# Two blocks of a two-layer network on one core: the scatter-adds of the second stretch read their row numbers from the loaded rows, loads run six blocks ahead instead of eight, and the last sum goes in two transfers instead of four

## The reference, cut to what matters

```
t = xf * rsqrt(mean(xf * xf) + EPS) * norm_w
vals, idx = top_k(t @ gate_w.T + gate_b, 4);  gates_k = softmax(vals)
h = einsum('mh,eoh->emo', t, w1) + b1          # 16 experts, 256 -> 512
a = minimum(h[..., ::2], 7);  b = clip(h[..., 1::2], -7, 7)
act = a * sigmoid(1.702 * a) * (b + 1)
y = einsum('emi,edi->emd', act, w2) + b2       # 256 -> 256
out = x + sum over the 4 experts of a token of gate * y
```

## Time and profile before

| | |
|---|---|
| time, median of 3 runs | 1045.91 us (1045.18 to 1046.28) |
| the profiled execution | 1043.59 us, of which its instructions span 1041.7 us |
| PE busy over the span | 970.5 us (93%) |
| POOL busy over the span | 427.1 us (41%) |
| second stretch on PE, first to last h_mm | 844.7 to 1010 us |

### The profile page before, as it was taken

One profiled execution on the slowest core, in us unless ns is written; L12 is line 12 of the kernel. 1 busy time (PEld: TensorE's weight loads), 2 busy tenths in 40 slices (PEclk: granted clock), 3 DMA queues, 4 the chain that ended last, 5 costly groups with the idle time before them and its releaser, 6 DMA issues.

```text
span 1041.7 us, 20507 instructions
## 1 busy us (share of the span) xinstructions
PE 970.5 (93%) x6020; PEld 820.9 (79%) x6020; DVE 722.6 (69%) x2545; ACT 671.3 (64%) x1944; POOL 427.1 (41%) x450
## 2 busy tenths in 40 slices
PE   6999999999999999999999999996888799999990
PEld 4669888887988888888888888884677689999980
DVE  3564775777677678677867867776867668888870
ACT  2657786687677767757866776782735456676650
POOL 3322431342362353154236225224064555665673
PEclk9999999999999999999999999998999899999995
DMA  9928993994789210020012004057177699998954
GB/s 307 307 80 301 376 371 113 375 377 164 278 293 376 96 62 1 18 88 31 1 62 73 2 1 165 3 183 264 52 188 169 188 247 217 225 226 215 225 133 81
DMA packets 93725, 180.53 MB, mean 173 GB/s; under 512 B 9949, under 2 KB 29085, under 8 KB 92717
## 3 DMA queue, kind: packets, MB, share of 16 engines
q1 hardware_dynamic: 73467, 148.55, 43.1%
q0 software_dynamic: 18800, 30.30, 12.9%
q10 hardware_dynamic: 1346, 0.36, 0.2%
HBM read 77.71 MB, written 107.99 MB: 178 GB/s over the span
## 4 chain that ended last, share of the span: by engine, by line
PE 86%; DVE 4%; issue 3%; ACT 2%; DMA 2%; POOL 1%; SPq 0%; ACTq 0%; DVEq 0%; POOLq 0%; another core or an unknown queue 0%
PE bank L1076 12%; PE bank L1040 11%; PE bank L1012 10%; PE bank L1085 6%; PE bank L1030 5%; PE bank L1002 5%; PE bank L991 4%; PE bank L962 3%; PE bank L868 3%; PE bank L1031 3%; PE bank L1001 3%; PE bank L1021 3%; PE bank L877 3%; PE bank L946 2%; PE bank L984 2%
## 5 line engine op out<-in xcount | busy, mean ns | idle before, releaser
L1076 PE MATMUL bank<-RB 128*128 128x128 f32 x1264 | 157.8, 279 | 6.1 <-issue 3.8
L1076 PEld LDWEIGHTS bank<-RB 128*128 128x128 f32 x1264 | 150.6, 195 | 9.6 <-issue 4.6
L1871 POOL TENSOR_TENSOR RB<-RB 128x512 f32<-128x512 f32 x64 | 67.6, 1056 | 203.1 <-DVE RB L1650 203.1
L1040 PE MATMUL bank<-RA,RB 128*128 128x256 f32 x512 | 133.7, 383 | 1.1 <-DVE X L1690 0.8
L1341 ACT ACTIVATE RB<-RA,nw 128x512 f32 x158 | 105.5, 715 | 37.2 <-issue 16.5
L1012 PE MATMUL bank<-RA 128*128 128x256 f32 x512 | 121.2, 380 | 0.0
L1012 PEld LDWEIGHTS bank<-RA 128*128 128x128 f32 x512 | 95.2, 190 | 15.0 <-issue 2.9
L1040 PEld LDWEIGHTS bank<-RA,RB 128*128 128x128 f32 x512 | 91.0, 190 | 15.5 <-issue 4.7
L1847 POOL TENSOR_TENSOR qs<-qs,half 128x4 f32<-128x4 f32 x64 | 64.9, 1014 | 93.1 <-DVE qs L1659 79.6
L1085 PE MATMUL bank<-RB,BC 128*128 128x256 f32 x316 | 83.2, 387 | 3.3 <-DVE BC L1777 2.3
L1242 ACT ACTIVATE RB<-bank 128x256 f32<-128x256 f32 x128 | 48.7, 381 | 57.9 <-PE bank L1031 52.8
(11 more groups left out here) (251 smaller groups left out, 2387.3 us busy)
## 6 DMA issues: line engine op xcount, KB each, us to landing
xsD<-BC SPq DMA_DIRECT2D x17, 4232.0 KB, 33.0
RB<-in_w2b SPq DMA_DIRECT2D x79, 256.0 KB
RB<-xsD SPq DMA_DIRECT2D x62, 264.5 KB
BC<-modD SPq DMA_DIRECT2D x16, 512.0 KB, 4.2
X<-xsD SPq DMA_DIRECT2D x17, 264.5 KB, 3.4
RA<-in_w SPq DMA_DIRECT2D x2, 2048.0 KB, 8.0
RA<-in_w SPq DMA_DIRECT2D x6, 512.0 KB, 11.5
RA<-in_L_attn_Wq SPq DMA_DIRECT2D x1, 2048.0 KB, 13.8
```

Source lines behind the costliest of these rows:

```text
L1040: m = pe.matmul(bank[5][:, t * 256:t * 256 + 256], OT[:, u % 2, t * 128:t * 128 + 128], Wo[:, h, :], start=(h == 0 and t == 0), stop=(h == ...
L1076: m = pe.matmul(ps[:, 128 * j:128 * j + 128], WS[:, n % 2, c, 128 * j:128 * j + 128], XT[:, n % 2, c * 128:c * 128 + 128], start=(c == 0), ...
L1871: pool.tensor_tensor(sq, qrow, qrow, ALU.mult).then_inc(mine("q_sq", p), 1)
```

## The change

In the second stretch `tok` is gone. `y_add` takes the token numbers straight from column 256 of the loaded rows. The rows' slot must then stay untouched until the add has read it and landed, so `xb(n)` now waits for `y_add(n - 11)` in place of `y_out(n - 11)` and `tok(n - 11)`, and the loads are listed six blocks ahead instead of eight. The first stretch keeps its copies. `merge` covers the same bytes in two transfers of 1 MB.

```diff
-    lo, hi, ahead = FIRST, NBLK, 8
+    lo, hi, ahead = FIRST, NBLK, 6
...
-        if lo <= n - 1 < hi:
-            p.add("tok", n - 1)
...
-    p.add("merge", by=16 * 4)
+    p.add("merge", by=16 * 2)
...
                     if n >= FIRST + RINGS[1]:
-                        on.wait_ge(*done("y_out", n - RINGS[1]))
-                        on.wait_ge(*done("tok", n - RINGS[1]))
+                        on.wait_ge(*done("y_add", n - RINGS[1]))
...
             def y_add(n):
                 on.wait_ge(*done("y_out", n))
-                on.wait_ge(*done("tok", n))
+                if n < FIRST:
+                    on.wait_ge(*done("tok", n))
+                else:
+                    on.wait_ge(*done("xb", n))
...
-                pool.indirect_dma_start((out_r, accD)[n % 2], bass.IndirectOffsetOnAxis(to[:, n % 6:n % 6 + 1], 0), YB[n % 5], None,
+                places = to[:, n % 6:n % 6 + 1] if n < FIRST else rows(n)[:, 256:257].bitcast(U32)
+                pool.indirect_dma_start((out_r, accD)[n % 2], bass.IndirectOffsetOnAxis(places, 0), YB[n % 5], None,
...
-                for i in range(4):
-                    pool.dma_start(out_r[512 * i:512 * i + 512, :].rearrange("(a c) n -> a (c n)", c=8), accD[512 * i:512 * i + 512, :].rearrange("(a c) n -> a (c n)", c=8),
+                for i in range(2):
+                    pool.dma_start(out_r[1024 * i:1024 * i + 1024, :].rearrange("(a c) n -> a (c n)", c=8), accD[1024 * i:1024 * i + 1024, :].rearrange("(a c) n -> a (c n)", c=8),
```

## The result

The changed kernel takes **1048.61 us** (median of 12 runs, 1046.62 to 1054.21), the kernel before 1045.07 (12 runs beside them, 1044.02 to 1047.83). The ratio is 1.0039, with a 95% interval of 1.0027 to 1.0050: about 4 us slower. (A ratio is taken over the timed runs as a whole. It is not the quotient of the two medians, and differs from it by up to 0.07%.) The profiled execution took 1048.47 us with a span of 1046.7. That of the kernel before took 1043.59, which is 1.5 us under the median of 1045.07, so the two profiles stand 4.9 us apart where the medians stand 3.5.

A forecast was written before the change was run, and what follows sets the result against it. It took the adds' chain of landings, then POOL's pace and the DMA-bound merge, as the bound. Terms -0.4 - 0.3 + 0.5 + 0.3 = +0.1, less half the even adds' small gains, gave 1045.7 us; range 1042.6 to 1049.4.

The forecast's parts named there:

- rival A: Second stretch: landings get slower as loads start together with adds; 0.2 us a step, 4.6 us, 1050.3 us; chance 0.23.
- The step by which A was to be told: Odd adds from block 27 to 71: 6.0 us a step and up would show rival A, 5.9 no change.
- What bounds the kernel: Blocks 27 to 73: add, landing, add, landing, twice side by side; then POOL's pace for five adds, then the merge.
- The six microseconds by which the last add stood behind the last y_out: Kernel's end: last y_out written 1014.66, last add starts 1020.68; taken as the adds' backlog, so the end hangs on them.
- The 2.73 us that an add takes "with the engines idle": Last add's landing time with idle engines, set against some 5 us in the loaded stretch.
- The new wait of SP: SP's row loads wait for an add's landing, some 3 us later each round; cost nothing, bounds 0 to 0.5 us.
- Where the loads' traffic goes: Last row loads run later, beside the last odd adds; 0.5 us lost, between 0 and 1.5.
- The tail: Adds 73 to 78 without copies, at 1.88 us start to start; together 0.4 us saved.
- The merge: Final sum in two transfers, first one slower to start; 0.3 us later, between -0.4 and +1.5.
- The first weights: Start of second stretch: asked for 2.2 to 2.4 us sooner, y_mm(21) loses its 0.28 us wait; 0.3 us saved.
- 6.0 and up is A: Sign in the profile: an odd adds' step of 6.0 us or more, block 27 to 71, means rival A.
- from 0.09 us a step on: Added time per odd adds' step, over 23 steps, from which rival A would decide the result.

The follow-up runs named there:

- e4_merge2: The kernel before with only the merge changed, to two transfers of 1 MB instead of four of 512 KB; 1044.17 us, ratio 0.9993.
- e7_three_targets: The changed kernel with second-stretch adds going in turn to three arrays, the third never summed; 1040.26 us against 1044.41, ratio 0.9967.
- e13: The changed kernel with thirteen row slots and the transposes of x in blocks 60 to 69 done three times over; 1045.23 us, ratio 1.0027.
- e15: The changed kernel with thirteen row slots and the transposes of x in blocks 50 to 69 done three times over; 1046.22 us, ratio 1.0047.
- e2_wait_add: The kernel before with row loads six ahead and waiting for y_add(n - 11) to land, copies and four merge transfers kept; 1050.16 us, ratio 1.0046.
- e1_ahead6: The kernel before with row loads six blocks ahead instead of eight, nothing else; 1046.37 us against 1044.81, ratio 1.0019.
- e3_slots13: The changed kernel with 13 row slots instead of 11, so loads wait for the add of block n - 7; 1045.04 us, ratio 1.0006.
- e12: The changed kernel with twelve row slots, rows seven ahead, five weight slots and w2x three ahead; 1044.29 us against 1042.04, ratio 1.0019.

## Why the prediction was wrong

It said 1045.7 us and no change that can be told; the kernel is 0.39% slower, in the manner of rival A, and near the size given there (4.6 us; some 4 measured). The step by which A was to be told has 6.11 - 5.89 = 0.22 in the two profiles, but 5.89 was a quick execution, and against the 6.00 of `e4_merge2` it is 0.11.

**What bounds the kernel** was read rightly: the adds' chain of landings, with PE near beside it. Loosening the chain gave 0.33 to 0.4% against before. But it was put too absolutely, and a view spoke against that: I read the end of the chain that ended last, and its stretch from 870 to 1005 us, which I did not weigh, is PE's. The six microseconds by which the last add stood behind the last y_out were read as backlog. 3.7 of them are there even where PE is the bound (1012.84 to 1016.56 in `e7_three_targets`), since the last five adds leave POOL 1.85 us apart; the backlog left at the end of the profile before was 2.3. And a backlog covers PE only until it is used up (e13, e15).

One reading of a row was wrong beside that. The 2.73 us that an add takes "with the engines idle" is the time of an add that moves nothing. In the kernel before, while adds 74 to 77 run:

```profile
1012.00:1020.00 8.00, 1.13 (x4) 0.68 (x4) 2.08 (x6) 0.00 (x0) 7.36 (x9) 0.69 0.04 1
```

1 GB/s is 8 KB in 8 us, where 128 rows of 1 KB would be 128 KB an add: these adds move no rows. So 2.73 against 5 compares idle with busy engines and no rows with 128, both at once.

**"The new wait of SP ... nothing, with 0 to 0.5 as bounds" is the step that failed.** The term stood at nothing, with PE's stalls as its only way to cost anything; the runs showed 0.27% (`e2_wait_add` against `e1_ahead6`) to 0.33% (the changed kernel against `e3_slots13`), some 3 us. Its mechanics were nearly right: a wait of 0.9 us in the mean and 1.7 at most on 34 loads (where I had said 1 to 4), some loads tight by tenths, h_mm(78) 1.9 us later in the stretch than before. What was missing is that a load held to the landing of so near an add makes the adds' chain slower:
- Near against far is 1.0039 and 1.0040 against 1.0006 and 1.0009, which is resolved. It is the distance to the add that is waited for that sets the loss.
- Stalls. With both loads on time the ratio was 1.0019 instead of 1.0039, a difference about as large as the two intervals' joint error (0.19%). Against stalls as the cause stands that the changed kernel's profile has a backlog in which they could be covered: its odd adds are 4.2 to 7.4 us behind y_out from block 41 to 73, and y_out(78) itself waits 2.28 us for a landing.
- The hold without a stall. It costs 0.13% over the far wait (e12 against e3), which is not resolved alone.

**"Where the loads' traffic goes"** had 0.5 us for the last loads only. This term was too small: six ahead alone, with no wait for a landing, cost 0.19% (0.07 to 0.31), 2.0 us. Before, the queue's wait for POOL released a load just after an add's issue (17.3 us in 23 places); with six ahead that wait is 0.7 us, and the weights' wait for PE sets the pace (36.5 us). The two other kernels with copies in which loads are not held by the add of five blocks before stand at 1.0014 and 1.0018. Three runs agree on 0.14 to 0.19%; all three keep the copies. The thirteen-slot kernel without them is paced by the weights' wait too and stands at 1.0006. Why this other timing is worse I can't show, since no trace here tells which packets of an add wait for which of a load.

**The small terms held.** The tail runs at 1.85 us a step instead of 1.92, and without a slow copy; with the merge in two about 0.1% came back (1.0006 against 1.0018, not resolved). The merge: nothing moves in the first 1.5 us, share 0.96, two landings at 8.0 and 12.3 us, 0.2 us saved in span where 0.3 of loss was entered. The first weights were asked for 6.82 us after the first row load (839.94 to 846.76) instead of 9.31, so 2.5 sooner, and y_mm(21) lost its wait, as said.

The account: +0.15 to 0.19% for loads six ahead, +0.27 to 0.33% for the near landing, -0.1% for copies and merge, 0.32 to 0.42% in all, against 0.39 measured. It is bookkeeping, since its terms come from the same few runs, and only the near landing and six ahead are resolved. Open is how the 0.3% divides between PE's stalls and longer landings: no run with a near wait is free of all other differences, and the intervals allow nearly all of it to either. Open too: the waits of single adds in one execution scatter by more than the effect (one kernel of median 1049.15 was profiled at 1043.59).

And the start: the profile before was taken from an execution 2.3 us under the median it was set against, with a step of 5.89, where `e4_merge2` shows 6.00. The sign "6.0 and up is A" would have named that kernel and `e3_slots13` too, which lose nothing. The bounds of rival A "from 0.09 us a step on" could not be read from one profile.

## What to carry to other kernels

When a buffer's release is moved from the issue of a transfer to its landing, count how many steps lie between that transfer and the load behind the wait: here seven or six cost nothing that could be told, five cost 0.3%. If slots can be had, buy the distance back before taking out the instruction that the wait hung on. When two chains run within a few per cent of each other and share the DMA engines, ask how large the backlog of one is, in more than one execution, before it is taken as cover for the other: up to its size a stall can be free, beyond it every stall counts in full, and it is not the same size in every execution. And with the same bytes in each round, still ask what the loads will now start together with.

## What the runs showed of the hardware

- An indirect add landed 2.7 us after its start with idle engines and no rows to move (share 0.04, 1 GB/s), and 4.8 to 6.0 us after it with 128 rows and the DMA engines at shares of 0.86 to 0.97; with the share at 0.44 it was 4.4 us. The next add that waited for the landing started 0.86 us after it.
- Halving one stream (215 to 177 GB/s in all) shortened the odd adds' step from 6.11 to 5.74 us and the kernel by 0.8% against the changed one, though PE, at 141.94 of 143 us, looked like the bound.
- A copy of 0.77 us on POOL behind an indirect add cost at most 0.07 us of POOL's pace (1.92 against 1.85, the latter with the numbers read from the loaded rows).
- 4.4 us more of PE's time cost 2.2 us (joint error 2.3) and 9.4 us more cost 4.3 (2.4), beside a chain of adds that in the two profiles stood 2.4 and 5.0 us behind PE's results just before, and 0.8 to 0.9 us behind them from block 59 to 71 (odd blocks).
- Two accumulating transfers of 1 MB instead of four of 0.5 MB ran at the same share and rate, 0.96 and 197 GB/s, and saved 0.2 us of span.
